# Four scale sums grouped into two steps, and a shorter lag before the next batch's layer-norm statistics, in a fused attention and adapter block

## The reference, cut to what matters

```python
h = _layernorm(x) * (1 + ca) + sa                     # x: 4 batches x 1024 tokens x 256
x = x + ga * attn(h)                                  # 16 heads of 16, softmax over 1024 keys
h = _layernorm(x) * (1 + cb) + sb
x = x + gb * ffn(h)
# inside ffn, for each batch of ffn: N = 8 experts
enc    = relu(h @ W_enc + b_enc)                      # 8 x 64 hidden
recon  = enc @ W_dec + b_dec
losses = mean((recon - h) ** 2)                       # one number for each expert
top1   = argmin(losses)                               # picks W_down, W_up
out    = h @ W_base + b_base + relu(h @ W_down + b_down) @ W_up + b_up
```

## Time and profile before

| | us |
|---|---|
| median of 3 runs | 996.22 |
| lowest, highest | 995.72, 997.45 |
| the profiled execution | 995.72 |
| its span, first to last instruction | 993.8 |
| mean granted clock of PE | 0.986 of full |

### The profile page before, as it was taken

The page is one execution under the profiler, slowest core; times in us unless marked ns, Lnnn a source line. Parts: engine busy times, 40 slices in busy tenths (PEclk is TensorE's granted clock), DMA queues, the critical chain, the costliest instruction groups (busy, mean ns, idle before and its releaser), DMA issues.

```text
span 993.8 us, 16502 instructions
## 1 busy us (share of the span) xinstructions
PE 955.0 (96%) x5794; PEld 478.0 (48%) x5794; DVE 801.2 (81%) x1631; ACT 659.7 (66%) x1295; POOL 332.2 (33%) x443
## 2 busy tenths in 40 slices
PE   6989999999899999999999999999999999999998
PEld 4444434344344445554454455444454455544476
DVE  4789989899688888878888888778788788888455
ACT  2138787888677867667668777766657766666830
POOL 4220234124365244011447433311257413116320
PEclk9879999999999999999999999998999999999999
DMA  6850051143450501453142511424333400132001
GB/s 177 142 95 26 12 104 50 49 104 79 74 97 12 100 32 34 76 85 92 55 113 39 86 46 36 84 33 91 100 92 60 68 30 25 39 97 78 29 6 48
DMA packets 47890, 66.93 MB, mean 67 GB/s; under 512 B 12139, under 2 KB 32112, under 8 KB 47796
## 3 DMA queue, kind: packets, MB, share of 16 engines
q1 hardware_dynamic: 46572, 65.00, 30.3%
q0 software_dynamic: 384, 0.79, 0.5%
q10 hardware_dynamic: 852, 0.09, 0.1%
HBM read 27.48 MB, written 12.59 MB: 40 GB/s over the span
## 4 chain that ended last, share of the span: by engine, by line
PE 80%; DVE 6%; ACT 5%; DMA 2%; POOL 2%; issue 2%; SPq 2%; ACTq 0%; DVEq 0%; POOLq 0%
PE pE L816 27%; PE pO L816 22%; PE pX L816 19%; PE pM L816 11%; DVE mx L1302 2%; ACT P L1123 2%; DMA QO<-lo 1%; ACT h1T L1164 1%; SPq L1886 1%; ACT h2f L1214 1%; DVE h2f L1461 1%; DMA P<-in_wmod 0%; DVE junk L1495 0%; DVE x L1392 0%; DMA QO<-mT 0%
## 5 line engine op out<-in xcount | busy, mean ns | idle before, releaser
L1302 DVE TENSOR_REDUCE mx<-pM 128x1 f32<-128x512 f32 x1006 | 630.6, 683 | 108.6 <-PE pM L816 103.6
L1123 ACT ACTIVATE P<-pE 128x512 f32<-128x512 f32 x995 | 524.6, 600 | 176.4 <-PE pE L816 173.3
L816 PE MATMUL pM<-KO,QO 48*128 48x512 f32 x1006 | 366.4, 453 | 6.2 <-DMA QO<-lo 3.4
L816 PE MATMUL pE<-QO,KO 50*128 50x512 f32 x995 | 347.4, 439 | 11.2 <-ACT h1T L1164 3.8
L816 PEld LDWEIGHTS pE<-QO,KO 50*128 50x128 f32 x995 | 164.8, 187 | 234.1 <-issue 128.3
L816 PE MATMUL pO<-P,V 128*17 128x512 f32 x2048 | 259.8, 602 | 5.2 <-ACT P L1123 5.1
L816 PEld LDWEIGHTS pM<-KO,QO 48*128 48x128 f32 x1006 | 163.9, 187 | 33.6 <-DVE mx L1302 20.7
L816 PEld LDWEIGHTS pO<-P,V 128*17 128x17 f32 x2048 | 40.4, 96 | 102.9 <-issue 88.8
L1711 POOL CAST mh<-mxc 128x16 fp32r<-128x16 f32 x32 | 6.4, 201 | 171.8 <-DVE mxc L1311 171.3
L816 PE MATMUL pX<-h1T,wqkv_s 128*128 128x512 f32 x112 | 58.8, 637 | 0.5 <-DVE acc L1495 0.4
L1770 POOL TENSOR_TENSOR Hs<-h2f,Hs 128x512 fp32r<-128x512 f32 x28 | 35.7, 1282 | 65.1 <-ACT Hs L1244 50.6
(11 more groups left out here) (308 smaller groups left out, 1051.8 us busy)
## 6 DMA issues: line engine op xcount, KB each, us to landing
outs<-osb SPq DMA_DIRECT2D x31, 256.0 KB, 2.4
KO<-hi SPq DMA_DIRECT2D x56, 128.0 KB, 4.0
QO<-hi SPq DMA_DIRECT2D x56, 128.0 KB, 5.5
x<-in_x SPq DMA_DIRECT2D x20, 256.0 KB, 3.6
out<-x SPq DMA_DIRECT2D x16, 256.0 KB, 2.1
AT<-outs SPq DMA_DIRECT2D x15, 256.0 KB
asum<-wsum SPq DMA_DIRECT2D x15, 256.0 KB
KO<-lo SPq DMA_DIRECT2D x28, 128.0 KB, 3.9
```

Source lines behind the costliest of these rows:

```text
L816: return e.matmul(o, lhsT, rhs, start=start, stop=stop)
L1123: e.activation(P[:, u % 3, j, :], bank(s), ACT.Exp).then_inc(*empties(s))
L1302: e.tensor_reduce(mx[:, hq % 2, k:k + 1, kh], bank(s), AX.X, ALU.max, negate=True).then_inc(*empties(s))
```

## The change

```diff
@@ plan
-            at(u + 2, ("prepb", b), ("wload", b), *(("sbc", b, i) for i in range(4)), ("scale", b))
+            at(u + 2, ("prepb", b), ("wload", b), ("sbc", b, 0), ("sbc", b, 1), ("scale", b))
@@ before
     if kind == "scale":
-        return [(("sbc", b, i), 0) for i in range(4)]
+        return [(("sbc", b, i), 0) for i in range(2)]
...
     if kind == "ln1s":
-        return [(("ln1load", b, a[0]), 2)]
+        return [(("ln1load", b, a[0]), 2 if b == 1 else 1.3)]
@@ vector, kind == "sbc"
-                    e.tensor_tensor_reduce(junk[:, 0:D], wd[:, i, 0:D], bc[:, 1, :], 1.0, 0.0, ALU.mult, ALU.add,
-                                           sbc[:, i:i + 1]).then_inc(*link.up())
+                    for p in (2 * i, 2 * i + 1):
+                        e.tensor_tensor_reduce(junk[:, 0:D], wd[:, p, 0:D], bc[:, 1, :], 1.0, 0.0, ALU.mult, ALU.add,
+                                               sbc[:, p:p + 1]).then_inc(*link.up())
+                        dve.wait_ge(*link.now())
```

## The result

The changed kernel takes 1004.33 us (median of 5 runs, 1002.44 to 1008.56) against 996.22 us: a ratio of 1.0083, 95% interval 1.0061 to 1.0104. It is 8 us slower, where +1.1 was forecast, and it lies above the range. Its profiled execution took 1006.59 us (span 1004.7, mean granted clock 0.981), 10.9 us more than the profiled one of before.

What follows compares the result with a forecast made beforehand. PE, busy 96% of the span, was taken to bound the kernel except where it waits for DVE. Terms 0 + 0.9 + 0.85 - 0.9 + 0 + 0.2 = +1.05 us gave 997.3 us, range 993.5 to 1000.4.

Steps and rivals of the forecast that it cites:

- the layer norms: Batches 2 and 3: statistics, transposition and `qk` come earlier, nobody waited for them; 0 us, range -1.0 to +1.5.
- one more wait for `h1T`: Batch 2's layer norm: one more transposition uses an E bank and the E behind it waits for ACT; +0.55 us.
- The -0.5: Layer norms: statistics that stood between reductions and an M move to a stretch with more room; -0.5 us.
- Batch 1: Sums near 477.92: no slack, two more sums delay the six reductions by 0.96 us; +0.9 us, range 0 to +1.0.
- Batch 2: Sums near 720.85: two more sums cost 0.96 us on DVE less 0.14 slack; +0.85 us taken, lower end 0.
- the first rival: Batch 2's later sums meet POOL and end with its subtraction: 1.8 instead of 0.85 us, total 998.4; chance 0.12.
- Batch 0: Sums near 237.70: up to 0.96 us delay, hidden by the wait for the DMA landing at 261.29; 0, range to +1.0.
- Batch 3's end: Attention's end: `scale` no longer meets POOL, two projections partly hide in PE's waits; -0.9 us, range -2.6 to +0.5.
- wait for `onorm`: Batch 3's end: `scale` on POOL now precedes `onorm`, so the first projection waits 0.4 to 1.1 us; +0.75 taken.
- SP: Copies into `KO` now stand ahead of `orow` on SP's queue, which just arrives in time; +0.2 us, range 0 to +2.
- The clock: Rival: one more half-clock stretch of 3.4 us, as near 690, 1000.7, chance 0.10; one fewer, 993.9, 0.08.

Runs made afterwards that it cites:

- e1: The changed kernel's sums grouped in all four batches, with the lag left at 2 units as in the kernel before: 997.89 us, ratio 1.0015.
- e7: The kernel before with the lag of 1.3 units in batch 3 alone, sums as before: 1000.23 us, ratio 1.0057.
- e4: The kernel before with only batch 1's sums grouped: 996.31 us, ratio 0.9998.
- e5: The kernel before with only batch 3's sums grouped: 996.35 us, ratio 0.9987.
- e6: The kernel before with the lag of 1.3 units in batch 2 alone, sums as before: 996.57 us, ratio 1.0007.
- e13: The kernel before with all four sums of batch 2 in one stretch, the next one with two PV: 997.55 us, ratio 1.0013.
- e14: The changed kernel with batch 3's second statistics a stretch later and the sums of batches 1 and 2 separate again: 997.74 us, ratio 1.0013.
- e17: A second profile, a single run, of the kernel with all sums grouped and the lag left at 2 units; its time is not given.
- e9: The kernel before with only batch 3's second statistics moved ahead of three reductions: 997.57 us, ratio 1.0019.
- e8: The changed kernel with batch 3's second statistics put back behind the next three reductions: 1001.33 us, ratio to before 1.0067.
- e12: The changed kernel with the loads of `orow` and `AT` ahead of the copies again in batches 2 and 3: 1004.80 us, ratio to before 1.0096.
- e16: Another profile of the changed kernel, a single run with nothing edited: 1002.53 us.
- e10: The changed kernel measured once more, nothing edited: 1005.29 us, ratio to before 1.0083.
- e11: The kernel before with one sum of batch 1 made five times instead of once: 999.09 us, ratio 1.0033.

## Why the prediction was wrong

- **The step that failed first** is the one on the layer norms, "I take 0". It asked whether anybody waited for what comes *earlier*, and nobody does. It didn't ask whether what the moved step itself waits for, the load of `xin`, comes earlier too. It doesn't. The rows were in reach in the trace of before (timelines of SP and DVE, and the landing time of this load alone, window 556:557.1); the last line is the same load in e1, where the statistics stand in their old place:

```profile
556.51 0.58 SPq L1954 DMA_DIRECT2D xin<-in_x  x1
...
562.62 0.75 DVE L1363 BATCH_NORM_STATS2 st<-xin 128x6 f32<-128x256 f32 x2
...
DMA to landing us min/median/max: 4.7/4.7/4.7
...
DMA to landing us min/median/max: 6.4/6.4/6.4
```

  In that trace DVE reads 6.1 us behind the issue and the load has landed after 4.7, so 1.4 us are to spare. The change moves the reader ahead by three reductions, 1.9 us, which gives a wait of 0.5 us: what e7 shows, where the load took 4.7 us again. The other seven profiles with the step moved have a load of 6.4 or 6.5 us and a wait of 1.3 to 1.5. That length isn't the change's doing: in e1, e4, e5, e6, e13, e14 and e17, with the step in its old place, the load took 6.4 or 6.5 us too, and DVE, 6.8 us behind the issue, came just late enough. So one trace of before gives the wait and a third of its size; several would have given all of it. Why the load takes 4.7 us in one execution and 6.5 in another stays open. Cost of the step: 1.1 us at full clock alone (e9), 2.2 in the changed kernel (e8) and 3.1 in the median there, and a low clock behind it in each of the changed kernel's profiles.
- **The rest of the layer norms** was to lie between -1.0 and +1.5. Batch 2 alone lost 1.6 us at full clock in the mean (e6) and 0.9 in the trace; batch 3 alone lost 2.5 (e7), of which the 1.1 of e9 is the one step. The one more wait for `h1T` came, but at 1.2 us instead of 0.55: 6.2 us, ten times, instead of 5.0, nine times. The -0.5 that I set against it wasn't seen. The last statistics move by three bursts in batch 2 and four in batch 3, not by one or two. What the rest of the loss is made of no run shows.
- **Batch 1**, +0.9: right, +0.8 to +1.2 where the clock stayed (e1, e4, e8, e12, e16, e17).
- **Batch 2**, +0.85: too small, and the first rival's 1.8 is what came (+1.7 to +2.4 in all profiles but e12, where the sums met POOL for less time, and e10, where a low clock followed). I had both rows of the kind, 1.39 and 1.23, and the new sums' neighbours on POOL, and still took the smaller value. The rule that the prediction names from the Trainium skill (page "SBUF — State Buffer", section "Who interferes with whom") agrees with four more rows, 1.38, 1.25, 0.71 and 1.37 us, and with e13, where the sums clear of POOL take 0.42.
- **Batch 0**, 0: about right. The bursts behind the sums came 0.5 us later (unit 66), and at unit 72 the changed kernel stands at +0.3 to +0.4 (e12, e16), but so do e4 and e6, +0.3 and +0.2, whose batch 0 is as before. What wasn't in the sum is PE's pause of 0.86 us and the low clock that follows it in 4 of 9 profiles.
- **Batch 3's end**, -0.9: -0.3 to -0.1 where the clock stayed. `scale` gave its 1.1 us and the projections were hidden in part, but most of it was lost again, and no run shows where. The sums stand two by two in two stretches here, with three reductions between (903.70 and 906.42 in the changed trace), not all four in one as in the other batches. The feared wait for `onorm` didn't come.
- **SP**, +0.2: the mechanism was right. `orow` was issued at 387.10 in the changed trace and DVE waited 0.6 us in each batch; e12 shows that it cost about nothing.
- **The clock** was one rival of 0.10 with no cause, and nothing in the sum. It was the larger part of the loss, 4.4 us in the mean beside 4.0 at full clock. e14 shows that it goes with the three places together; the rest of its cause is open. The sum should have priced each place where DVE newly holds PE twice, once for its length and once for its chance of a half-clock stretch, which cost 1.6 us at batch 1's sums (2.7 less 1.1) and 3.3 at batch 2's in e10 (5.3 less 2.0).

## What to carry to other kernels

When a step is moved earlier, look at its inputs as well as at its readers: take the slack between the landing of that very load and its first read, from more than one profile, and compare it with the distance moved. And where PE runs near its limit, a new pause of 1 us can cost more than 1 us, since a stretch at half clock may follow; so count the new pauses, not only their sum.

## What the runs showed of the hardware

- Behind new pauses of PE of 0.4 to 1.4 us the granted clock fell to half in some executions and not in others with the same pause: behind batch 1's sums (0.4 to 0.7 us idle) in 3 profiles of 9, at batch 2's layer norm (1.2 us) in 1 of 9, behind batch 3's statistics (1.1 us) in 7 of 7. It also fell where PE hadn't stood at all but was paced by DVE, at 908 in the changed kernel. It came back while PE was busy throughout, after 3.4 us at batch 1's sums and after 10 us in e11.
- One load of 256 tokens (256 KB), with six copies issued just ahead of it and six behind, landed after 4.7 us in three profiles, 5.4 in one and 6.4 to 6.5 in fourteen; the median of its tile was 2.9 us in the changed kernel.
- A sum over two SBUF tensors of 128x256, 0.42 us alone, took 0.71 to 1.39 us beside instructions of POOL, and POOL's cast took 0.88 instead of 0.62 us beside the sums.
